# Layer 1 of a two-layer network: feed-forward over four chunks with its weights stationary, the softmax division moved into it, and single-bank maxima in attention

## The reference

```python
# attention, 16 heads of 32 channels
q, k, v = (proj(wq), proj(wk), proj(wv))
q, k = apply_rope(q, k, sin, cos)
att = jnp.einsum('bhqd,bhkd->bhqk', q, k) * (1.0 / math.sqrt(HD))
att = jax.nn.softmax(att, axis=-1)
y = jnp.einsum('bhqk,bhkd->bhqd', att, v)
return y @ wo.T
# feed-forward, 512 -> 1408 -> 512
gate = _qlinear(x, wq_gate, s_gate)      # x @ ((wq - 128) * scale).T
gate = jax.nn.silu(gate)
up = _qlinear(x, wq_up, s_up)
return _qlinear(gate * up, wq_down, s_down)
```

## Time and profile before

| | us |
|---|---|
| three runs | 3289.12, 3297.5, 4808.1 (median 3297.5) |
| the profiled execution's own time | 3295.37 |
| its span, first to last instruction | 3292.0 |
| attention of layer 1, with its preparation | about 1256 to 2634 |
| feed-forward of layer 1, with its preparation | about 2634 to 3292 |
| mean granted TensorE clock (1 is 2.4 GHz) | 0.949 |

### The profile page before, as it was taken

One profiled execution on the slowest core, in us unless ns is written; L12 is line 12 of the kernel. 1 busy time (PEld: TensorE's weight loads), 2 busy tenths in 40 slices (PEclk: granted clock), 3 DMA queues, 4 the chain that ended last, 5 costly groups with the idle time before them and its releaser, 6 DMA issues. The chain is left out here.

```text
span 3292.0 us, 56401 instructions
## 1 busy us (share of the span) xinstructions
PE 2926.6 (89%) x19876; PEld 2109.3 (64%) x19876; DVE 1971.3 (60%) x2924; ACT 1277.8 (39%) x1987; POOL 1324.0 (40%) x971
## 2 busy tenths in 40 slices
PE   5999999199999984799999999999999659999999
PEld 4888888078888873555555555555554248888887
DVE  4666665767777753676666666666666234444444
ACT  2111111066666651254544555455554412222222
POOL 1111010322333320377777777777777812112111
PEclk9999999599999996799999999999999979999999
DMA  2100000312222223111211111121111042212211
GB/s 83 33 32 32 32 32 20 118 52 96 96 90 82 99 74 113 52 54 63 65 59 59 64 58 59 58 65 58 59 59 33 13 184 74 70 64 72 72 64 51
DMA packets 97053, 215.00 MB, mean 65 GB/s; under 512 B 11408, under 2 KB 27792, under 8 KB 96400
## 3 DMA queue, kind: packets, MB, share of 16 engines
q1 hardware_dynamic: 95472, 210.14, 19.1%
q10 hardware_dynamic: 1440, 2.76, 0.2%
...
## 5 line engine op out<-in xcount | busy, mean ns | idle before, releaser
L1134 DVE TENSOR_REDUCE l_attn_maxima<-l_attn_ps_max 128x2 f32<-128x1024 f32 x512 | 618.6, 1208 | 229.7 <-PE l_attn_ps_max L1188 229.6
L1101 POOL TENSOR_TENSOR l_attn_summed<-l_attn_summed,l_attn_probs 128x1024 f32<-128x1024 f32 x256 | 600.4, 2379 | 132.6 <-ACT l_attn_probs L1052 132.5
L1052 ACT ACTIVATE l_attn_probs<-l_attn_ps_sc 128x1024 f32<-128x1024 f32 x512 | 496.7, 1022 | 274.1 <-PE l_attn_ps_sc L1177 271.5
L1101 POOL TENSOR_TENSOR l_attn_summed<-l_attn_probs 128x1024 f32<-128x1024 f32 x128 | 302.0, 2381 | 304.7 <-ACT l_attn_probs L1052 304.7
L70 PE MATMUL l_ffn_ps_gu<-l_ffn_w_gu,l_ffn_xt 128*128 128x512 f32 (+1 forms) x1536 | 345.0, 377 | 46.8 <-DMA l_ffn_xt<-xt_chunks 46.8
L61 PE MATMUL l_attn_ps_prep<-l_attn_wqkv_hi,l_attn_xt 128*128 (+1 forms) x1024 | 301.5, 378 | 74.7 <-DMA l_attn_xt<-xt_chunks 55.2
L70 PEld LDWEIGHTS l_ffn_ps_gu<-l_ffn_w_gu,l_ffn_xt 128*128 128x128 f32 x1536 | 279.1, 189 | 87.2 <-DMA l_ffn_xt<-xt_chunks 48.3
L1367 POOL TENSOR_TENSOR l_ffn_mixed<-l_ffn_gate,l_ffn_up 128x512 f32<-128x512 f32 (+1 forms) x96 | 115.1, 1199 | 521.8 <-DVE l_ffn_up L1416 473.5
L1188 PE MATMUL l_attn_ps_max<-l_attn_qk_hi 32*128 32x512 f32 x1024 | 252.6, 488 | 71.4 <-DVE l_attn_maxima L1134 71.3
L1188 PEld LDWEIGHTS l_attn_ps_max<-l_attn_qk_hi 32*128 32x128 f32 x1024 | 98.7, 189 | 281.7 <-DVE l_attn_maxima L1134 204.8
L1198 PE MATMUL l_attn_ps_y<-l_attn_probs,l_attn_v 128*32 128x512 f32 x2048 | 278.0, 616 | 1.1 <-ACT l_attn_probs L1052 1.1
...
## 6 DMA issues: line engine op xcount, KB each, us to landing
l_attn_xt<-xt_chunks SPq DMA_DIRECT2D x128, 512.0 KB, 3.3
...
l_attn_xin<-in_x SPq DMA_DIRECT2D x32, 256.0 KB, 2.7
s<-l_attn_s_sb SPq DMA_DIRECT2D x32, 256.0 KB, 2.0
l_ffn_xa<-in_x SPq DMA_DIRECT2D x32, 256.0 KB, 2.7
l_ffn_xb<-in_x SPq DMA_DIRECT2D x32, 256.0 KB, 2.9
l_ffn_s_sb<-s SPq DMA_DIRECT2D x32, 256.0 KB, 4.0
```

Source lines behind the costliest of these rows:

```text
L1052: act.activation(probs[kt % RING][:, hs, :], ps_sc[:, hs, :], ACT.Exp, scale=ATT_SCALE).then_inc(exp_done, 1)
L1101: pool.tensor_tensor(total[:, hs, :], old[:, hs, :], probs[kt % RING][:, hs, :], ALU.add).then_inc(added, 1)
L1134: dve.tensor_reduce(maxima[b][:, j, PAIR * hp:PAIR * hp + PAIR, half:half + 1], ps_max[:, :, :], AX.X, ALU.max).then_inc(max_read, 1)
```

## The change

In the attention:
- `xt` has four buffers instead of two, and SP's order in a tick is written out: the stores stand between the loads, at the places where what they wait for is due.
- `ps_max` is two tiles of one bank. A `maximum` is one head: one matmul, one DVE reduction over 128x512, 64 to a unit instead of 32 of twice the size. A matmul waits for the reduction two before it.
- On TensorE an even step does the value products of the two steps before it, with two maxima between them; an odd step does none.
- ACT: the evacuation of a projection comes between the two halves of the next even step's exponentials, and no longer after its own step.
- No reciprocal and no multiplication: numerator and denominator are both copied and stored (`den_out`, a new array in device memory).

In the feed-forward:
- A tick is a block of four chunks. `xt` is one tile for 512 tokens, loaded by four transfers whose runs are 128 numbers long, and only when the last up product of the block before is done. The weights are stationary and the tokens move past them: for each of 11 slices of 128 hidden channels 8 matmuls for gate and 8 for up, 512 wide. The hidden values come out transposed, so the 352 transposes are gone.
- A channel's scale is now one number to a partition, loaded as 128x11: gate's goes into the silu on ACT, up's into one `scalar_tensor_tensor` on DVE that also multiplies gate and up. ACT copies the high part, POOL subtracts the low part.
- DVE takes the reciprocals of the denominators (4 to a chunk), POOL multiplies y with them.
- The down products of a block come after all 11 slices; the output projections stand after slices 4, 6, 8 and 10.
- The first block's tokens and the first two chunks' y and denominators are loaded in the preparation, behind the weights.
- The loop holds two blocks to an iteration (ticks 2 to 7), after two that are written out.

```diff
-        xt = two("xt", [P, 2, KD, P], F32R)
+        xt = [sb(f"xt{i}", [P, 2, KD, P], F32R) for i in range(XTS)]
...
-        ps_max = ps("ps_max", [P, PAIR, DIM])
+        ps_max = [ps(f"ps_max{i}", [P, DIM]) for i in range(2)]
...
-        FIRST_LATE, LAST_QB0 = 10, 19
-        TURNS_FOR = {0: 2, 8: 3, 12: 4}
-
-        def maxes(t, s):
-
-            first = 2 * s + FIRST_LATE
-            return [(t - 1 + i // N_MAX, 1 - i // N_MAX, i % N_MAX) for i in (first, first + 1) if live(t - 1 + i // N_MAX, NT)]
+        FIRST_LATE, LAST_QB0 = 20, 39
+        TURNS_FOR = {0: 2, 16: 3, 24: 4}
+
+        def maxes(t, s, p, slots):
+
+            found = []
+            for slot in slots:
+                i = HPG * s + FIRST_LATE + slot
+                late = 1 - i // N_MAX
+                if live(t - late, NT):
+                    found.append((t - late, parity(p, late), i % N_MAX))
+            return found
...
+            def load(m, c):
+                if live(m, NT):
+                    b = c % XTS
+                    src = m // GROUPS * CPB + c
+                    need(sp, proj_done, CPB * m + c - XTS + 1)
+                    sp.dma_start(fp32(xt[b][:, :, :, :]).rearrange("p h k n -> p (h k n)"),
+                                 xt_in[src if isinstance(m, int) else sp.snap(src)]).then_inc(xt_ld[b], 16)
...
+            def tick(t, p):
+                load(t, 0)
+                store(t - 2, 0, y_copied, y_sb, yt_out)
+                load(t, 1)
+                load(t, 2)
+                load(t, 3)
+                store(t - 2, 0, den_read, den_sb, den_out)
+                load(t, 4)
+                load(t, 5)
+                load(t, 6)
+                store(t - 2, 1, y_copied, y_sb, yt_out)
+                load(t, 7)
+                store(t - 2, 1, den_read, den_sb, den_out)
...
@@ scalar, tick @@
+            def tick(t, p):
+                for s in range(STEPS):
+                    weigh(t, s, 0)
+                    if s % 2 == 0:
+                        evacuate(t, p, s - 1)
+                    weigh(t, s, 1)
+                    if s % 2 == 0:
+                        evacuate(t, p, s)
...
@@ gpsimd, tick @@
-                    for qb, at in ((0, 7), (1, 15)):
-                        if s == at and live(t - 2, NT):
-                            g = QB * (t - 2) + qb
-                            need(pool, y_copied, g + 1)
-                            need(pool, inverted, PIECES * (g + 1))
-                            pool.tensor_tensor(y_sb[qb][:, :], y_sb[qb][:, :], inv_den[:, :], ALU.mult).then_inc(y_ready, 1)
...
@@ vector, tick @@
-                    for qb, at in ((0, 3), (1, 11)):
-                        if at <= s < at + PIECES and live(t - 2, NT):
-                            g = QB * (t - 2) + qb
-                            cols = slice(DIM // PIECES * (s - at), DIM // PIECES * (s - at + 1))
-                            need(dve, den_read, g + 1)
-                            dve.reciprocal(inv_den[:, cols], inv_den[:, cols]).then_inc(inverted, 1)
...
@@ vector, maximum @@
-                dve.tensor_reduce(maxima[b][:, j, PAIR * hp:PAIR * hp + PAIR, half:half + 1], ps_max[:, :, :], AX.X, ALU.max).then_inc(max_read, 1)
+                dve.tensor_reduce(maxima[b][:, j, h, half:half + 1], ps_max[i % 2][:, :], AX.X, ALU.max).then_inc(max_read, 1)
...
@@ tensor, maximum @@
-                need(pe, max_read, N_MAX * m + i)
+                need(pe, max_read, N_MAX * m + i - 1)
+                r = head(h)
+                pe.matmul(ps_max[i % 2][:, :], qk_hi[b][r, 0, P * j:P * j + P], qk_hi[b][r, 1, DIM * half:DIM * half + DIM],
+                          start=True, stop=True, skip_group_check=True).then_inc(max_done, 1)
...
@@ tensor, tick @@
             def tick(t, p):
                 for s in range(STEPS):
                     m, qb, kt = quad(t, s)
-                    todo = [(u, parity(p, back), i) for u, back, i in maxes(t, s)]
                     if live(m, NT):
                         scores(m, parity(p, 0 if s < CPB else 1), qb, kt)
-                    if todo:
-                        maximum(*todo[0])
-                    if event(t, s):
-                        prepare(t, p, s)
-                    if s % 2:
-                        for a in todo[1:]:
+                    if s % 2 == 0:
+                        values(t, p, s - 2)
+                    for a in maxes(t, s, p, (0, 1)):
+                        maximum(*a)
+                    if s % 2 == 0:
+                        values(t, p, s - 1)
+                        for a in maxes(t, s, p, (2,)):
                             maximum(*a)
-                    m, qb, kt = quad(t, s - 1) if s else quad(t - 1, STEPS - 1)
-                    if live(m, NT):
-                        pv(m, parity(p, 0 if s <= CPB else 1), qb, kt)
-                    if s % 2 == 0:
-                        for a in todo[1:]:
+                        if event(t, s):
+                            prepare(t, p, s)
+                        for a in maxes(t, s, p, (3,)):
+                            maximum(*a)
+                    else:
+                        if event(t, s):
+                            prepare(t, p, s)
+                        for a in maxes(t, s, p, (2, 3)):
                             maximum(*a)
...
@@ layer1_ffn @@
+        def load_xt(sp, t):
+            for i in range(CB):
+                src = CB * t + i
+                sp.dma_start(fp32(xt[:, :, :, P * i:P * i + P]),
+                             xt_in[src if isinstance(t, int) else sp.snap(src)].rearrange("p (h k n) -> p h k n", h=2, k=KD)).then_inc(xt_ld, 16)
...
+                load_y(t, 2)
+                load_y(t, 3)
+                load_x1(t, 0)
+                load_x1(t, 1)
+                load_y(t + 1, 0)
+                load_y(t + 1, 1)
+                if live(t + 1, BLOCKS):
+                    need(sp, up_done, KH * (t + 1))
+                    load_xt(sp, t + 1)
+                store(t, 0)
+                load_x1(t, 2)
+                store(t, 1)
+                load_x1(t, 3)
+                store(t, 2)
+                store(t, 3)
...
+                    pool.tensor_tensor(ht_lo[:, j, :], mixed[b][:, :], fp32(ht_hi[:, j, :]), ALU.subtract).then_inc(ht_lo_ready, 1)
+                        pool.tensor_tensor(yt[y][:, :, :], yt[y][:, :, :], den[y][:, :, :], ALU.mult).then_inc(y_scaled, 1)
...
+                        act.activation(gate[b][:, :], ps_gate[b][:, :], ACT.Silu, scale=sc_gate[:, j:j + 1]).then_inc(silu_done, 1)
+                        act.activation(ht_hi[:, j - 1, :], mixed[(p + j - 1) % 2][:, :], ACT.Copy).then_inc(ht_hi_ready, 1)
...
+                    dve.scalar_tensor_tensor(out=mixed[b][:, :], in0=ps_up[b][:, :], scalar=sc_up[:, j:j + 1], in1=gate[b][:, :],
+                                             op0=ALU.mult, op1=ALU.mult).then_inc(mixed_ready, 1)
+                    if j < 2 * CB:
+                        y, c = j // 2 % 2, CB * t + j // 2
+                        need(dve, yt_den_ld[y], 32 * (CB // 2 * t + j // 4 + 1))
+                        for g in (2 * (j % 2), 2 * (j % 2) + 1):
+                            dve.reciprocal(den[y][:, g, :], den[y][:, g, :]).then_inc(inverted, 1)
...
+            def product(out_bank, w, j):
+                for k in range(KD):
+                    for half in range(2):
+                        mm = pe.matmul(out_bank[:, :], w[:, k, P * j:P * j + P], xt[:, half, k, :], start=(k == half == 0), stop=(k == KD - 1 and half == 1))
+                return mm
+
+            def tick(t, p):
+                for j in range(KH):
+                    n, b = KH * t + j, (p + j) % 2
+                    if j == 0:
+                        need(pe, xt_ld, 16 * CB * (t + 1))
+                    need(pe, silu_done, n - 1)
+                    product(ps_gate[b], w_gate, j).then_inc(gate_done, 1)
+                    need(pe, mixed_ready, n - 1)
+                    product(ps_up[b], w_up, j).then_inc(up_done, 1)
+                    if j in S_AFTER:
+                        i = S_AFTER[j]
+                        c, y = CB * t + i, i % 2
+                        need(pe, yt_hi_ready, c + 1)
+                        need(pe, yt_lo_ready, c + 1)
+                        need(pe, s_ready, c - 1)
+                        three_pass(pe, ps_s[y][:, :], lambda k: yt_hi[y][:, k, :], lambda k: yt_lo[y][:, k, :],
+                                   lambda k: wo_hi[:, k, :], lambda k: wo_lo[:, k, :], KD, s_done)
+                for i in range(CB):
+                    c, cols = CB * t + i, slice(P * i, P * i + P)
+                    need(pe, scaled, c - 1)
+                    need(pe, ht_lo_ready, KH * (t + 1))
+                    two_pass(pe, ps_down[i % 2][:, :], lambda k: ht_hi[:, k, cols], lambda k: ht_lo[:, k, cols],
+                             lambda k: w_down[:, k, :], range(KH), True, True).then_inc(down_done, 1)
```

417 lines of the change are left out of this document (185 added, 232 removed).

## The result

The changed kernel takes 3192.4 us (median of four runs, 3188.86 to 3199.31), against 3293.0 for the kernel before beside it (median of three): a ratio of 0.9697, 95% interval 0.9671 to 0.9722. One execution of the kernel before (4808 us) and one of the second experiment (5755 us) were disturbed and are left out of all medians. The forecast was 3179 us with a range of 3140 to 3235. The profiled execution has a span of 3187.1 us where the sum said 3176, so 105 us went and 116 were expected.

A forecast was written before the change was run, and what follows sets the result against it. TensorE was taken as the bound, with waits as gaps in the attention. From 3292.0 us: attention's loop -70, outside it -10 and -4, feed-forward -32, giving 3176; with 3.4 beyond the span, 3179 us, range 3140 to 3235.

The forecast's parts named there:

- the pair of steps: Attention's loop on TensorE: an even and an odd step without waits go from 8.43 to 8.78 us, summed from pieces.
- Waits for the maxima against switches: Attention's loop: single banks remove 57 us of waits for reductions; more changes of tile shape add 39 us.
- Waits for xt: Attention's loop: earlier loads and four buffers remove 34.2 us of TensorE's waits and 18 us of slow clock.
- Jumps back unchanged: Attention's loop: the six jumps back, 1.93 us and a slow clock behind them, stay, since the matmuls are the same.
- Outside the loop: Attention: -10 us for reductions waited for in ticks 0, 1 and 16; -4 for the last unit's four reciprocals.
- Feed-forward: Gate, up and transposes -38 us; start of down products +2; last chunk's end +1; loop's jumps +3: -32 us.
- Rival 3: Feed-forward: stationary weights cost more; at 0.25 us a matmul instead of 0.2275 nothing is gained, about 3211 us; chance 0.04.
- Rival 1: Attention: two heads' maxima no longer run side by side, +77 us less what was idle, about 3250 us; chance 0.12.
- Rival 2: Feed-forward: next block's xt comes late, PE waits 9 us seven times and slows down, about 3255 us; chance 0.05.
- Rival 4: Attention: DVE becomes the bound if a 512-wide reduction costs what a 1024-wide one does, about 3380 us; chance 0.03.
- Rival 5: Attention: the order does nothing for the waits, each maximum waiting for its own reduction; about 3220 us; chance 0.08.
- Preparation: Before the feed-forward: changed loads let PE start from 5 us earlier to 7 later; taken as 0.

The follow-up runs named there:

- the second experiment: One of the twelve follow-up kernels; the text does not settle which, so its change and median cannot be given. Its disturbed execution took 5755 us.
- the experiment's own: Changed kernel with everything in the attention as before, save that the division has moved to the feed-forward: 3215.4 us, ratio 0.9777 to the kernel before.

## Why the prediction was right, and where it was off

- **Bound and mechanism.** Right: TensorE is the engine to save on, and both kinds of wait went. So was the estimate for the reduction (0.68, measured 0.686). That the pair of steps came out as worked out (8.78, measured 8.79) is luck: its parts are off by up to 0.30 us each and cancel (+0.22, +0.24 and +0.10 against -0.25 and -0.30).
- **Waits for the maxima against switches, -57 + 39 = -18 us.** The direction is right, the net gain was put too high: 19.8 us in the loop, of which some 10 are the experiment's own, so about 10. Neither the 57 nor the 39 was measured by itself.
- **Waits for xt, -34 - 18 = -52 us.** The step that failed is the reason: the working put it down to SP's new order and the four buffers, and the experiment with two buffers and the old order has no wait either. What did it is the division's move. The size was nearly right, about 47 us. Both terms show in the rows: the 34.2 us of waits are gone, and TensorE's busy time in the 14 ticks, for the same matmuls, falls from 1021.8 to 1003.0 us while the granted clock rises from 0.97 to 0.99, so the slow clock had cost some 18.8. What the sum left out is that other waits take some of it back: with the division alone moved, TensorE waits 4.5 us more for `qk_lo` (16.7 instead of 12.2) and 1.1 more at the jumps, beside what it waits longer for the maxima. The gain fell wholly on the seven ticks with a long stop (4.0 us on average): they took 81.3 us and take 75.9. The six ticks with a jump, which held 6 us of short waits for `xt`, take 79.0 and 79.1.
- **The loop as a whole, -70 us.** Measured -56.6. The difference of 13 is, by these estimates, 5 for `xt` and 8 for the maxima.
- **Jumps back unchanged.** Off by 3.4 us in the recorded stop. That the stop was one of DVE as well as of TensorE could not be read from the earlier trace rows.
- **Outside the loop, -14 us.** Measured -14.9, and that it fits is luck. Ahead of the loop 10 were expected and 4.8 measured, behind it 4 and 10.1; and the part ahead takes 146.2 us or 153.9 in executions of the same attention, where the kernel before took 150.7.
- **Feed-forward, -38 + 2 + 1 + 3 = -32 us.** Measured -27.4, by two misses that partly cancel. "Stationary weights cost nothing" holds: with the tiles back in their old places the stage takes 578.5 us, 40 less than before and so 8 better than forecast. What was missed is the layout: 13 us in the stage (1.76 a block), caused by two tiles of 44 bytes. Rival 3 named the symptom, slower matmuls, with another reason and about four times the size (0.25 us against 0.2275; measured 0.2325 against 0.2267). The start of the down products (+2) was right, 8 x 0.24; the jumps (+3) cost nothing.
- **Jumps in the feed-forward.** No row shows a stop at a jump of the new feed-forward. The Trainium skill (Runtime: NRT & Kernel Launch, "Instruction fetch mechanics") gives TensorE room for 2048 instructions; by that rule 1248 do not stop, and the trace agrees (blocks of 72.92 to 72.94 us, with a jump and without).
- **Rivals.** Rival 1: heads still start together; beside it, by the Trainium skill (TensorE: Matmul & The Clock Gate, "The cost: per-tile semaphore tail") four more increments a pair would make it 8.89 us, where the trace has 8.79; since the 8.78 fits by luck, this does not settle an increment's price. Rival 2: no wait for the next block's `xt`. Rival 4: DVE is busy for 69% of a tick. Rival 5: the waits are gone.
- **Preparation.** 34.1 us instead of 38.7, inside the -5 to +7.
